# Feed-forward of a quantised transformer block on one core: one more tile of look-ahead, four slots for the first-layer values, norm moved off VectorE, steps reordered

## The reference

```
def act_quant(x):
    s = 127.0 / jnp.clip(jnp.max(jnp.abs(x), axis=-1, keepdims=True), EPS)
    xq = jnp.clip(jnp.round(x * s), -128, 127) / s
xn = adaln(x, c, g2, w_ada2, b_ada2)      # x * rsqrt(mean(x*x)+eps) * g * (1+scale) + shift
h = jax.nn.gelu(bitlinear(xn, w_fc1, b_fc1), approximate=False)     # 512 -> 2048
x = x + bitlinear(h, w_fc2, b_fc2)                                  # 2048 -> 512
```

## Time and profile before

| | us |
|---|---|
| median of three executions | 3425.88 |
| the profiled execution, its own time | 3427.46 |
| its span in the trace | 3425.7 |
| of it, the feed-forward stage (from the barrier at 3065.4 to the end) | 360 |

### The profile page before, as it was taken

How to read it: one execution, slowest core, us unless ns; L and a number is a source line. 1 busy time by engine, 2 the same in 40 slices (tenths; PEclk the granted TensorE clock), 3 DMA queues, 4 the chain that set the end, 5 groups by cost and what they waited for, 6 DMA issues and landing times. The chain is left out here.

```text
span 3425.7 us, 69821 instructions
## 1 busy us (share of the span) xinstructions
PE 3035.3 (89%) x21846; PEld 1423.6 (42%) x21846; DVE 2382.4 (70%) x4529; ACT 1709.2 (50%) x2150; POOL 1949.8 (57%) x1631
## 2 busy tenths in 40 slices
PE   2799989999999989999489979997999799956887
PEld 1344434444444434444234434443444344423444
DVE  6367774776557764677577787778777877737997
ACT  5135541555225532455255556555555555545776
POOL 1047850788137860688348775787588657842221
PEclk6899999999999999999789999999899899988999
DMA  7312301222112212122222213221223122133000
GB/s 301 112 36 50 108 26 38 48 47 90 53 29 47 64 66 50 39 47 74 83 47 57 46 60 82 47 61 54 73 47 80 47 66 50 41 126 126 24 28 31
DMA packets 93499, 222.71 MB, mean 65 GB/s; under 512 B 20544, under 2 KB 22592, under 8 KB 92144
## 3 DMA queue, kind: packets, MB, share of 16 engines
q1 hardware_dynamic: 91104, 211.78, 22.2%
q0 software_dynamic: 2192, 8.39, 0.6%
HBM read 84.80 MB, written 33.60 MB: 35 GB/s over the span
## 5 line engine op out<-in xcount | busy, mean ns | idle before, releaser
L604 DVE TENSOR_REDUCE b_mxs<-ps 128x1 f32<-128x512 f32 x1024 | 659.3, 686 | 252.5 <-PE ps L494 224.1
L604 DVE TENSOR_REDUCE a_mxs<-ps 128x1 f32<-128x512 f32 x1024 | 659.2, 686 | 235.4 <-PE ps L494 212.0
L577 ACT ACTIVATE a_p<-ps 128x1024 f32<-128x1024 f32 x512 | 500.4, 1019 | 346.4 <-PE ps L508 345.5
L577 ACT ACTIVATE b_p<-ps 128x1024 f32<-128x1024 f32 x512 | 500.6, 1019 | 334.1 <-PE ps L508 332.0
L467 POOL TENSOR_TENSOR b_sum<-b_p 128x512 f32<-128x512 f32 x384 | 502.9, 1310 | 132.5 <-ACT b_p L577 132.5
L467 POOL TENSOR_TENSOR a_sum<-a_p 128x512 f32<-128x512 f32 x384 | 498.9, 1300 | 133.5 <-ACT a_p L577 133.5
L494 PE MATMUL ps<-b_k,b_q 96*128 96x512 f32 x1024 | 436.4, 466 | 22.9 <-DVE b_mxs L604 9.3
L494 PE MATMUL ps<-a_k,a_q 96*128 96x512 f32 x1024 | 431.4, 465 | 6.0 <-DVE a_xv L926 3.4
L523 PE MATMUL ps<-b_p,b_vx 128*32 128x512 f32 x2048 | 387.5, 610 | 23.7 <-POOL b_sum L472 16.3
L523 PE MATMUL ps<-a_p,a_vx 128*32 128x512 f32 x2048 | 382.3, 601 | 23.7 <-POOL a_sum L472 21.2
L525 PE MATMUL ps<-b_sum,b_unit 128*32 128x512 f32 x768 | 384.9, 609 | 0.0
(11 more groups left out here) (201 smaller groups left out, 3934.5 us busy)
## 6 DMA issues: line engine op xcount, KB each, us to landing
a_q<-a_qh SPq DMA_DIRECT2D x128, 128.0 KB, 2.3
a_k<-a_kh SPq DMA_DIRECT2D x128, 128.0 KB, 2.4
b_q<-b_qh SPq DMA_DIRECT2D x128, 128.0 KB, 2.3
b_k<-b_kh SPq DMA_DIRECT2D x128, 128.0 KB, 2.3
p_wf<-in_w_fc SPq DMA_DIRECT2D x8, 1024.0 KB, 21.2
a_kl<-in_x SPq DMA_DIRECT2D x4, 2048.0 KB, 8.5
a_q<-a_ql SPq DMA_DIRECT2D x64, 128.0 KB, 2.3
a_k<-a_kl SPq DMA_DIRECT2D x64, 128.0 KB, 2.3
```

Of the source, the lines that this page charges most:

```text
L577: act.activation(self.p[:, s % self.NP, :], self.st[:, 2 * (s % 2):2 * (s % 2) + 2, :].rearrange("p a n -> p (a n)"), ACT.Exp, scale=self. ...
L604: dve.reduce_max(self.mxs[:, c:c + 1], self.mx[c % 2], axis=AX.X).then_inc(self.s_mxr, 1)
```

## The change

- `norm` is split: `x_scale` on ACT (x times 1/rms, a Copy with a per-row scale), then `modulate` on POOL (times gain), then `shift` and `bias` on POOL as before. They run at offset 5, a tile earlier than norm did; the first scales, `x_round`, `x_bits`, `x_transpose`, `fc1`, `hidden` each move one tile ahead as well.
- `h` has four slots, so the loop's body becomes four steps (6 turns; before 13 turns of two).
- `hidden` works on two PSUM banks at once: two DVE instructions of 1024 columns in place of four of 512. `fc1` then waits for banks in pairs.
- PE order in step n: x_transpose(3), fc1(3), h_transpose(0), fc2(0).
- ACT order in step n: gelu(1), h_round(0), x_copy(3), x_scale(5), x_round(4), h_copy(0).
- DVE: maximum(0) is followed by its clip before the x chain's maximum; the small operations interleave; norm is gone.
- The wait for x beyond the first batch moves from DVE to ACT, the wait for w2 to PE's first fc2.

```diff
-    FIRST, AHEAD = -4, 4
-    LOOPS = (N - 1 - AHEAD) // 2
+    FIRST, AHEAD = -5, 5
+    UNROLL = 4
+    LOOPS = (N - 1 - AHEAD) // UNROLL
-        h = sb("h", [P, 2, FF], FP32)
+        h = sb("h", [P, UNROLL, FF], FP32)
...
+                def modulate(n, r):
+                    pool.wait_ge(s_xn, n + 1)
+                    pool.tensor_tensor(tk[:, r % 2, :], tk[:, r % 2, :], mt(n, 0), ALU.mult).then_inc(s_xm, 1)
                 def shift(n, r):
-                    pool.wait_ge(s_xn, n + 1)
+                    pool.wait_ge(s_xm, n + 1)
...
-                steps(pool, ((4, shift), (4, bias)))
+                steps(pool, ((5, modulate), (5, shift), (5, bias)))
...
-                        pe.wait_ge(s_h, 4 * n + j + 1)
+                        if j % 2 == 0:
+                            pe.wait_ge(s_h, 2 * n + j // 2 + 1)
...
-                steps(pe, ((-1, fc2), (2, x_transpose), (2, fc1), (0, h_transpose)), lambda: pe.wait_ge(s_w2, 16))
+                steps(pe, ((3, x_transpose), (3, fc1), (0, h_transpose), (0, fc2)))
...
+                def x_scale(n, r):
+                    if not isinstance(n, int) or n >= 2:
+                        act.wait_ge(s_q[0], n - 1)
+                    act.activation(tk[:, r % 2, :], xt(n), ACT.Copy, scale=rs[:, bass.ds(n, 1)]).then_inc(s_xn, 1)
...
-                steps(act, ((0, h_round), (2, x_copy), (1, gelu), (3, x_round), (0, h_copy)))
+                steps(act, ((1, gelu), (0, h_round), (3, x_copy), (5, x_scale), (4, x_round), (0, h_copy)), all_x)
...
-                def norm(n, r):
-                    if not isinstance(n, int) or n >= 2:
-                        dve.wait_ge(s_q[0], n - 1)
-                    dve.scalar_tensor_tensor(tk[:, r, :], xt(n), rs[:, bass.ds(n, 1)], mt(n, 0),
-                                             ALU.mult, ALU.mult).then_inc(s_xn, 1)
...
                 def hidden(n, r):
                     done(0, n, 3)
-                    for j in range(4):
-                        dve.wait_ge(s_f1, 4 * n + j + 1)
-                        cols = slice(j * HALF, (j + 1) * HALF)
-                        dve.scalar_tensor_tensor(h[:, r, cols], f1[:, j, :], col(0, 3, n), b1[:, cols],
-                                                 ALU.mult, ALU.add).then_inc(s_h, 1)
+                    if not isinstance(n, int) or n >= 3:
+                        dve.wait_ge(s_q[1], n - 2)
+                    for c in range(2):
+                        dve.wait_ge(s_f1, 4 * n + 2 * c + 2)
+                        cols = slice(c * 2 * HALF, (c + 1) * 2 * HALF)
+                        dve.scalar_tensor_tensor(h[:, r, cols], f1[:, 2 * c:2 * c + 2, :].rearrange("p a n -> p (a n)"),
+                                                 col(0, 3, n), b1[:, cols], ALU.mult, ALU.add).then_inc(s_h, 1)
...
-                steps(dve, ((0, maximum(1)), (3, maximum(0)), (0, clipped(1)), (3, clipped(0)), (0, inverse(1)), (3, inverse(0)),
-                            (0, factor(1)), (3, factor(0)), (2, x_bits), (1, hidden), (0, h_bits), (4, norm), (-1, residual)), all_x)
+                steps(dve, ((0, maximum(1)), (0, clipped(1)), (4, maximum(0)), (0, inverse(1)), (4, clipped(0)), (0, factor(1)),
+                            (4, inverse(0)), (4, factor(0)), (3, x_bits), (2, hidden), (0, h_bits), (-1, residual)))
```

More of the change, by code:

```diff
@@ L1415, in layer1b @@
         s_v = [sem(f"v_chain{i}") for i in range(2)]
-        s_xn, s_xs, s_xb = sem("xn"), sem("xs"), sem("xb_ok")
+        s_xn, s_xm, s_xs, s_xb = sem("xn"), sem("xm"), sem("xs"), sem("xb_ok")
         s_sc, s_rnd, s_q = ([sem(f"{a}{i}") for i in range(2)] for a in ("sc", "rnd", "q"))
@@ L1426, in step @@
                     if every or 0 <= n + o < N:
-                        f(n + o, (r + o) % 2)
+                        f(n + o, (r + o) % UNROLL)
             for n in range(FIRST, 1):
-                step(n, n % 2, False)
+                step(n, n % UNROLL, False)
             before_loop()
             with eng.Fori(0, LOOPS) as i:
[L1432 to L1435, removed]
+                for r in range(UNROLL):
+                    step(UNROLL * i + 1 + r, (1 + r) % UNROLL, True)
+            for n in range(1 + UNROLL * LOOPS, N + 1):
+                step(n, n % UNROLL, False)
         with nc.Block() as block:
@@ L1464, in _ @@
                 pool.wait_ge(s_b, 32)
+                def modulate(n, r):
+                    pool.wait_ge(s_xn, n + 1)
+                    pool.tensor_tensor(tk[:, r % 2, :], tk[:, r % 2, :], mt(n, 0), ALU.mult).then_inc(s_xm, 1)
                 def shift(n, r):
-                    pool.wait_ge(s_xn, n + 1)
-                    pool.tensor_tensor(tk[:, r, :], tk[:, r, :], mt(n, 1), ALU.add).then_inc(s_xs, 1)
+                    pool.wait_ge(s_xm, n + 1)
+                    pool.tensor_tensor(tk[:, r % 2, :], tk[:, r % 2, :], mt(n, 1), ALU.add).then_inc(s_xs, 1)
                 def bias(n, r):
                     pool.tensor_tensor(xt(n), xt(n), b2[:, :], ALU.add).then_inc(s_xb, 1)
-                steps(pool, ((4, shift), (4, bias)))
+                steps(pool, ((5, modulate), (5, shift), (5, bias)))
             @block.tensor
@@ L1481, in x_transpose @@
                     for k in range(KC):
-                        mm = pe.transpose(xt_ps[:, k * P:(k + 1) * P], xq[:, r, k * P:(k + 1) * P], identb)
+                        mm = pe.transpose(xt_ps[:, k * P:(k + 1) * P], xq[:, r % 2, k * P:(k + 1) * P], identb)
                     mm.then_inc(s_xt, 1)
@@ L1487, in fc1 @@
                     for j in range(4):
-                        pe.wait_ge(s_h, 4 * n + j + 1)
+                        if j % 2 == 0:
+                            pe.wait_ge(s_h, 2 * n + j // 2 + 1)
                         for k in range(KC):
-                            mm = pe.matmul(f1[:, j, :], xqT[:, r, k, :], w1[:, k, j * HALF:(j + 1) * HALF],
+                            mm = pe.matmul(f1[:, j, :], xqT[:, r % 2, k, :], w1[:, k, j * HALF:(j + 1) * HALF],
                                            start=k == 0, stop=k == KC - 1)
@@ L1498, in h_transpose @@
                             pe.wait_ge(s_hc, 2 * n + k // 8 + 1)
-                        mm = pe.transpose(ht_ps[k // 8][:, k % 8 * P:(k % 8 + 1) * P], hq[:, r, k * P:(k + 1) * P], identb)
+                        mm = pe.transpose(ht_ps[k // 8][:, k % 8 * P:(k % 8 + 1) * P], hq[:, r % 2, k * P:(k + 1) * P], identb)
                         if k % 8 == 7:
@@ L1503, in fc2 @@
                 def fc2(n, r):
+                    if isinstance(n, int) and n == 0:
+                        pe.wait_ge(s_w2, 16)
                     pe.wait_ge(s_o, n + 1)
@@ L1507, in fc2 @@
                             pe.wait_ge(s_hc, 2 * n + k // 8 + 1 + 2)
-                        mm = pe.matmul(f2, hT[:, r, k, :], w2[:, k, :], start=k == 0, stop=k == FC - 1)
+                        mm = pe.matmul(f2, hT[:, r % 2, k, :], w2[:, k, :], start=k == 0, stop=k == FC - 1)
                     mm.then_inc(s_f2, 1)
-                steps(pe, ((-1, fc2), (2, x_transpose), (2, fc1), (0, h_transpose)), lambda: pe.wait_ge(s_w2, 16))
+                steps(pe, ((3, x_transpose), (3, fc1), (0, h_transpose), (0, fc2)))
             @block.scalar
@@ L1517, in _, with all_x @@
                 act.sem_inc(s_hc, 2)
+                act.wait_ge(s_rs, 1)
+                act.wait_ge(s_x[0], 16)
+                def all_x():
+                    for b in range(1, B):
+                        act.wait_ge(s_x[b], 16)
+                def x_scale(n, r):
+                    if not isinstance(n, int) or n >= 2:
+                        act.wait_ge(s_q[0], n - 1)
+                    act.activation(tk[:, r % 2, :], xt(n), ACT.Copy, scale=rs[:, bass.ds(n, 1)]).then_inc(s_xn, 1)
                 def x_round(n, r):
                     act.wait_ge(s_sc[0], n + 1)
-                    act.activation(tk[:, r, :], tk[:, r, :], ACT.Identity, bias=MAGIC, scale=col(0, 2, n)).then_inc(s_rnd[0], 1)
+                    act.activation(tk[:, r % 2, :], tk[:, r % 2, :], ACT.Identity, bias=MAGIC, scale=col(0, 2, n)).then_inc(s_rnd[0], 1)
                 def x_copy(n, r):
                     act.wait_ge(s_xt, n + 1)
-                    act.activation(xqT[:, r, :, :].rearrange("p k t -> p (k t)"), xt_ps[:, 0:D], ACT.Copy).then_inc(s_xtc, 1)
+                    act.activation(xqT[:, r % 2, :, :].rearrange("p k t -> p (k t)"), xt_ps[:, 0:D], ACT.Copy).then_inc(s_xtc, 1)
                 def gelu(n, r):
                     for c in range(2):
-                        act.wait_ge(s_h, 4 * n + 2 * c + 2 + 4)
+                        act.wait_ge(s_h, 2 * n + c + 1 + 2)
                         part = h[:, r, c * 2 * HALF:(c + 1) * 2 * HALF]
@@ L1539, in h_copy @@
                         act.wait_ge(s_ht, 2 * n + c + 1)
-                        act.activation(hT[:, r, 8 * c:8 * c + 8, :].rearrange("p k t -> p (k t)"), ht_ps[c], ACT.Copy).then_inc(s_hc, 1)
```

(30 more changed lines are left out.)

## The result

The changed kernel takes 3448.62 us (median of five, 3441.09 to 3449.12) beside 3425.88 (median of five, 3422.83 to 3428.38); the ratio is 1.0061, with a 95% interval of 1.0046 to 1.0075. A second set of five, taken later beside others, gave 3445.14, ratio 1.0059 (1.0045 to 1.0073). The forecast was 3446.3, 0.6% slower. The profiled execution had 3448.62 with a span of 3446.8, 21.1 us more than that of before; the forecast of the span was 3446.1.

A forecast was written before the change was run, and what follows sets the result against it. Bound before: a 9.80 us ring over PE and ACT; after, one over ACT of 10.44. Steps 17.9, start 3.2, end and rounding -0.7 make plus 20.4 on 3425.9: 3446.3 us, own range 3442 to 3450.

The forecast's parts named there:

- The bound of before: Last stage: a closed ring of waits over PE and ACT, 9.80 us a step, sets the pace; DVE, 93.4% busy, follows.
- TensorE's ring: h_copy, fc2, x_transpose, x_copy, fc1, h_transpose: 9.80 us a step, the same cycle under the new PE list.
- ScalarE's ring: h_copy, gelu, h_round, x_copy, then fc1 to the next h_copy: 10.44 us a step, 0.64 more each.
- What was costed at nothing: In the steps: DVE's lighter load, x_scale (0.6 to 0.71 us), modulate (1.27 us), fc1's paired waits, all off the ring.
- The start: Stage start: one more fc1 and longer POOL work put the first h_copy at 3123.1 instead of 3119.91, 3.2 us lost.
- 1.5 of possible half clock: At the stage's start: an early fc1 running partly at clock 0.50 could add 1.5 us, as an upper bound.
- The end: From tile 28's h_copy: 21.8 us to the last h_copy, then 8.9 to the span's end; -0.7 us with rounding.
- Same time: Rival: gelu and h_round fit into ACT's 3.14 us, so PE's 9.81 us steps stay; 3428.7 us; 8%.
- VectorE as limit: Rival: DVE at 93% is the true limit, so less work on it shortens each step; 3401 us; 5%.
- The clock in the steps: Rival: the clock falls in longer PE pauses, fc1 takes 5.13 instead of 3.63 us each step; 3488 us; 5%.
- The loop's turns: Rival: the longer loop body stalls at its turns, five at 2.2 us, 11 us in all; 3457 us; 8%.

The follow-up runs named there:

- e5: Kernel before with only norm split (x_scale on ScalarE, modulate on GpSimd, norm gone from VectorE); 3428.0 us, ratio 1.0008.
- e1: Changed kernel with only ScalarE's order turned, gelu moved behind x_copy; 3430.7 us, ratio 1.0018 to the kernel before.
- e6: Changed kernel with TensorE's list written as before and the wait for w2 ahead of the loop; 3446.9 us, ratio 1.006 to the kernel before.
- e2: Kernel before with only ScalarE's order turned as the change has it, gelu first; 3504.1 us, ratio 1.0229.
- e3: Changed kernel with the second gelu call over 512 of its 1024 columns; 3433.6 us, ratio 1.0026 to the kernel before.
- e4: Changed kernel with the second gelu call over 64 of its 1024 columns; 3428.0 us, ratio 1.0006 to the kernel before.
- e7: Changed kernel with x_transpose one turn ahead of its fc1 and the x chain one tile further ahead; 3409.7 us, ratio 0.9954 to the kernel before.

## Why the prediction was right, point by point

The mechanism was the one forecast; that the sum met the span to 0.7 us (3446.1 and 3446.8) is in part luck. The steps gave 17.5 us where 17.9 were summed, the end 0.5 more than forecast, and the first profile is the only one of five with this start that has fc1 of tile 3 at full clock. The executions of the changed kernel lie 8 us apart.

- **The bound of before.** The chain of waits was the right view and the busy shares the wrong one. e5 shows it: 7 us in 100 taken off the busiest engine left the steps at 9.81.
- **TensorE's ring is unchanged by the new list.** Shown by e1: 9.81 with the new list and everything else changed. e6 shows that the list makes no difference where ScalarE's ring is the longer one.
- **ScalarE's ring of 10.44.** Measured 10.45 in the loop. The terms, forecast and found: h_copy 1.82 and 1.82, gelu 1.89 and 1.90, h_round 1.89 and 1.89, x_copy to h_copy 4.84 and 4.84. h_round's 1.89 was the one chosen between bounds; it overlaps its follower by 0.11 as the others do. The order as cause is shown by e1 and e2, the size by e3 and the floor by e4.
- **What was costed at nothing.** It did cost nothing in the steps. x_scale took 0.73, just over my upper bound of 0.71. The two-bank hidden took 2.38 to 2.39 for both halves (2.4 expected). VectorE's idle time before h_bits is 1.8 us a step (some 2 expected). The one thing that I didn't see is a collision of GpSimd with VectorE, told below. In the steps modulate begins 0.08 us behind the end of h_bits (3297.63 and 3297.55), so there they don't meet, and only just. At the start, where they did meet, the first h_copy came 33.4 us after the first modulate, 0.2 off the forecast's 33.6.
- **The start.** 3.2 us forecast, 3.1 in the first profile and 4.6 in the second. The 1.5 of possible half clock, carried in the range only, came in the second and in e3, e4 and e6: it is the more frequent case, and the forecast's middle value left it out.
- **The end.** 30.7 us from h_copy(28) forecast, 31.2 and 30.8 measured. Here too an fc2 took longer than its 3.61: that of tile 30 in the first profile (5.30 us, granted clock 0.67 over it) and that of tile 29 in the second (4.90). Only the first reached the end, with 0.4 us.
- **The rivals.** Same time (gelu and h_round fit): excluded by the trace of the changed kernel. VectorE as limit: excluded by e5. The clock in the steps: stayed at 1.00. The loop's turns: steps at the turns of the loop are as long as the others within 0.02 us (10.44 to 10.46), and in 285 us three packets came on the queue q8, against one in 270 us before. By the Trainium skill's rule ("Runtime: NRT & Kernel Launch", "Instruction fetch mechanics") a body that no longer fits would have stalled at each turn; this one, four steps long, shows no stall. Why one packet more or less comes isn't shown.

The spread of the changed kernel's times (3441 to 3449) isn't fully explained: the profiles show two parts of it, the first clock levels and the start of the stage. The first norm or modulate moves by up to 6 us over the profiles of all kernels (3084.09 to 3090.01), though no edit touches what stands ahead of the stage.

## What to carry to other kernels

A software pipeline on in-order engines has one ring for every pair of engines that hand a tile back and forth; write each as a sum of starts and put, for every engine, all that stands in its queue between the two hand-overs into it. In these runs moving work off the busiest engine left the step as it was (e5), and so did the deeper look-ahead (e1): neither shortened the longest ring; ScalarE with 70% busy set the pace here through two instructions on the wrong side of one copy. Once the rings were written down, moving x_transpose and its copy away from its consumer, and h_round ahead of gelu, made the kernel 0.8% faster than the one before, where the change had lost 0.6%.

## What the runs showed of the hardware that was not expected

GpSimd and VectorE hold each other up in some pairs of instructions. In the changed kernel's start modulate took 2.20 us in place of 1.27, when it met h_bits, and in e7 h_bits took 2.02 in place of 1.23, when it met modulate; the shift behind waited in its turn:

```profile
3119.83 1.22 DVE L1624 TENSOR_SCALAR c_hq<-c_h 128x2048 bf16<-128x2048 f32 x1
3119.97 2.20 POOL L1469 TENSOR_TENSOR c_tk<-c_tk,c_mod_r 128x512 f32<-128x512 f32 x1 [3.01 <-ACT c_tk L1536]
```
```profile
3120.87 1.27 POOL L1469 TENSOR_TENSOR c_tk<-c_tk,c_mod_r 128x512 f32<-128x512 f32 x1 [2.29 <-ACT c_tk L1536]
3121.20 2.02 DVE L1624 TENSOR_SCALAR c_hq<-c_h 128x2048 bf16<-128x2048 f32 x1
3122.22 2.13 POOL L1473 TENSOR_TENSOR c_tk<-c_tk,c_mod_r 128x512 f32<-128x512 f32 x1
```

Take h_bits in e7: it ends at 3123.22, and modulate ahead of it ended at 3122.14, so that about 1.1 us are left for h_bits from there, near its usual length. In the other case modulate ends 1.12 us after h_bits (3122.17 and 3121.05), and the shift of e7 1.13 after it. Who started first finished first, and the other took from there its own length less some 0.15. A short overlap costs less: in e7's steps modulate met only the end of h_bits, the last 0.4 us, and took mostly 1.53 to 1.56, 1.70 at most. The maximum over the same tile, on the other hand, ran beside GpSimd's work throughout at its usual 2.28. The Trainium skill, "SBUF — State Buffer", section "SBUF: two separate sides", says that the two engines share a pair of ports under an exclusive lock, for VectorE's instructions in a two-port mode or with two SBUF inputs (these only against a GpSimd instruction that reads SBUF). The traces agree in that h_bits blocks and is blocked and the maximum isn't. No view shows the mode itself, but h_bits works off its 2048 columns in 1.23 us and the maximum its 2048 in 2.28. In the steps of the changed kernel they did not meet: modulate's mean from 3140 to 3400 is 1.273 us, its longest 1.28.
